# Tables and value/gate weights prepared behind the first queries and keys of an attention and expert layer, with queries and keys one slot earlier in the written order

## What is computed

```python
x = x + attn(layernorm(x), Wqg, Wkv, Wout)      # 16 heads, keys of 16, values of 64
x = x + ffn(layernorm(x), gate_kernel, gate_bias, w_gate, w_up, w_down, sw_gate, sw_up, sw_down)

# attn: q, k, v are L2-normed per head
q, g = split(x @ Wqg); k, v = split(x @ Wkv)
aggr = square(relu(q @ k.T)) @ v
out = tanh(|aggr|) * aggr / |aggr| * tanh(silu(g)); return out @ Wout
# ffn: 16 experts of 64, top 4 out of the best 2 of 4 groups, scaled by 2.5, and one shared expert of 128
y = sum_e combine[e] * ((silu(x @ w_gate[e]) * (x @ w_up[e])) @ w_down[e]) + shared(x)
```

## Time and profile before

| | us |
|---|---|
| median of 3 runs | 763.42 (762.53 to 763.88) |
| the profiled execution | 764.07 |
| its span, first to last instruction | 762.0 |
| PE busy in the span | 675.1 |
| DVE busy | 542.9 |
| ACT busy | 434.9 |
| POOL busy | 354.8 |
| mean granted clock of PE | 0.973 |

### The profile page before, as it was taken

The page is one execution under the profiler, slowest core; times in us unless marked ns, Lnnn a source line. Parts: engine busy times, 40 slices in busy tenths (PEclk is TensorE's granted clock), DMA queues, the critical chain, the costliest instruction groups (busy, mean ns, idle before and its releaser), DMA issues.

```text
span 762.0 us, 15278 instructions
## 1 busy us (share of the span) xinstructions
PE 675.1 (89%) x5160; PEld 519.9 (68%) x5160; DVE 542.9 (71%) x1739; ACT 434.9 (57%) x986; POOL 354.8 (47%) x368
## 2 busy tenths in 40 slices
PE   2658888999999999999999999999999999998876
PEld 1525456777777777777777778777777777666775
DVE  3526657788796868787886868687877968686652
ACT  3456757666567575666666675656566675543211
POOL 3225746464546454555546464554545463734000
PEclk9879999999999999999999999999999999999998
DMA  8699486657291929357481909284572919000000
GB/s 211 109 139 105 90 92 110 72 96 92 72 116 37 121 32 137 51 104 86 86 102 57 124 19 143 36 129 59 103 80 79 102 56 120 6 15 3 7 8 8
DMA packets 72830, 61.24 MB, mean 80 GB/s; under 512 B 8625, under 2 KB 72497, under 8 KB 72753
## 3 DMA queue, kind: packets, MB, share of 16 engines
q1 hardware_dynamic: 72752, 60.26, 53.8%
HBM read 41.37 MB, written 18.87 MB: 79 GB/s over the span
## 4 chain that ended last, share of the span: by engine, by line
PE 50%; DVE 27%; ACT 11%; issue 7%; DMA 3%; POOL 1%; SPq 1%; DVEq 0%; ACTq 0%; POOLq 0%
PE ps_a L493 9%; PE ps_f L437 9%; PE ps_f L418 8%; PE ps_f L355 5%; PE ps_s L464 4%; PE ps_f L357 4%; PE ps_f L356 4%; DVE it L841 4%; DVE norms_y L652 3%; DVE norms_t L651 3%; PE ps_f L397 3%; ACT qk_parts L546 2%; ACT r L592 2%; DMA qkt<-qk_rows 2%; ACT qk_sq L548 2%
## 5 line engine op out<-in xcount | busy, mean ns | idle before, releaser
L324 POOL TENSOR_TENSOR p<-r 128x512 f32<-128x512 f32 x256 | 264.2, 1053 | 322.9 <-ACT r L592 290.0
L592 ACT ACTIVATE r<-ps_s 128x512 f32<-128x512 f32 x256 | 139.6, 601 | 86.8 <-PE ps_s L464 83.0
L493 PE MATMUL ps_a<-p,v 128*64 128x256 f32 x1024 | 147.9, 400 | 4.0 <-POOL p L324 2.3
L493 PEld LDWEIGHTS ps_a<-p,v 128*64 128x64 f32 x1024 | 65.0, 138 | 45.2 <-POOL p L324 5.2
L584 ACT ACTIVATE it<-ps_f 128x256 f32<-128x256 f32 x144 | 55.6, 386 | 63.4 <-PE ps_f L357 60.3
L887 DVE TENSOR_TENSOR big<-ps_a,wt 128x256 f32<-128x256 f32 x128 | 53.7, 420 | 48.5 <-ACT big L601 47.2
L841 DVE TENSOR_TENSOR it<-ps_f,it 128x256 f32<-128x256 f32 x144 | 58.8, 419 | 28.9 <-ACT it L584 28.3
L464 PE MATMUL ps_s<-qkt 64*128 64x256 f32 x512 | 66.7, 335 | 9.4 <-DMA qkt<-qk_rows 7.4
L730 DVE TENSOR_REDUCE norms_m<-sq 128x8 f32<-128x512 f32 x64 | 43.7, 683 | 43.7 <-ACT sq L556 43.7
L437 PE MATMUL ps_f<-wdown,it 128*128 128x128 f32 x576 | 72.6, 288 | 1.3 <-DVE it L858 1.3
L437 PEld LDWEIGHTS ps_f<-wdown,it 128*128 128x128 f32 x576 | 70.0, 203 | 1.5 <-DVE it L858 1.5
(11 more groups left out here) (153 smaller groups left out, 1487.9 us busy)
## 6 DMA issues: line engine op xcount, KB each, us to landing
qk_rows<-qk_parts SPq DMA_DIRECT2D x16, 1024.0 KB, 4.4
qkt<-qk_rows SPq DMA_DIRECT2D x64, 256.0 KB, 9.9
qkt<-qk_rows SPq DMA_DIRECT2D x128, 128.0 KB, 9.3
x_in<-in_L_attn_tokens SPq DMA_DIRECT2D x16, 128.0 KB, 3.4
x_res<-in_L_attn_tokens SPq DMA_DIRECT2D x16, 128.0 KB, 14.1
out<-o_sb SPq DMA_DIRECT2D x16, 128.0 KB, 14.2
big<-in_L_attn_Wqg SPq DMA_DIRECT2D x1, 640.0 KB, 4.2
big<-in_L_attn_Wkv SPq DMA_DIRECT2D x1, 640.0 KB, 5.5
```

The costliest lines, as they stand in the source:

```text
L324: pool.tensor_tensor(p[h % 4][:], r[h % 2][:], r[h % 2][:], ALU.mult).then_inc(probs_done, 1)
L493: last = pe.matmul(ps_a[k % 2][64 * e:64 * e + 64, 0:N], v[s % 3][:, t, h * DV:(h + 1) * DV], p[h % 4][:, t * N:(t + 1) * N], start=(t == ...
L592: act.activation(r[h % 2][:], ps_s[h % 2][:], ACT.Relu).then_inc(relu_done, 1)
```

## The change

PE's list: in slot 5 qk 0 takes the place of v 0 (place 26, bank 2). In slot 6 qk 1 and v 0 take places 29 (bank 1) and 30 (bank 2), v 1 takes 32 (bank 0). In slot 7 v 2 takes 34 (bank 2); v 3 stays at 36. x2T, at 38, now shares its bank with v 2, v 0 with qk 0. DVE's order follows: low part 0 in slot 5, low part 1 and sums 0 and 1 in slot 6, sums 2 and 3 in slot 7.

At the start PE and ACT wait for less (the identity, one constant; Wqg and Wkv each under a semaphore of its own). POOL builds the other nine tables in slot 1 of step -2, behind its first root. ACT copies the high parts of value and gate weights behind the evacuation of qk 1 of step -2. DVE makes the low parts of query and key weights behind xn, those of value and gate weights in slot 6 behind low part 1, followed by the cast of sel. PE waits for all tables at the head of step -1, ACT behind its copies.

```diff
--- before.py
+++ after.py
@@ -48,9 +48,9 @@
         [("P", "g", 2), ("F", "gu", 5), ("F", "cT", 0), ("F", "gu", 6), ("O", "rT", 0)],
         [("O", "rB", 0), ("O", "rB", 1), ("F", "gu", 7), ("O", "rB", 2), ("L", "xT", 0), ("O", "rB", 3), ("P", "g", 3),
          ("F", "gu", 8)],
-        [("O", "y", 0), ("L", "v", 0), ("O", "y", 1), ("F", "cB", 0)],
-        [("L", "v", 1), ("L", "qk", 0), ("F", "cB", 1), ("L", "v", 2), SKIP],
-        [("L", "qk", 1), ("F", "cB", 2), ("L", "v", 3), ("F", "cB", 3), ("O", "x2T", 0), SKIP],
+        [("O", "y", 0), ("L", "qk", 0), ("O", "y", 1), ("F", "cB", 0)],
+        [("L", "qk", 1), ("L", "v", 0), ("F", "cB", 1), ("L", "v", 1), SKIP],
+        [("L", "v", 2), ("F", "cB", 2), ("L", "v", 3), ("F", "cB", 3), ("O", "x2T", 0), SKIP],
     ]
     ORDER = [job for slot in FILL for job in slot]
     assert len(FILL) == SLOTS and len(ORDER) % 4 == 0
@@ -166,7 +166,7 @@
 
 
         x_loaded, x_back = ([sem(f"{name}{q}") for q in range(2)] for name in ("x_loaded", "x_back"))
-        w_loaded = [sem(f"w_loaded{k}") for k in range(3)]
+        w_loaded = [sem(f"w_loaded{k}") for k in range(4)]
         c_loaded = sem("c_loaded")
         out_stored = sem("out_stored")
         consts_pool, consts_dve = sem("consts_pool"), sem("consts_dve")
@@ -215,7 +215,7 @@
 
             load_x(0, 0)
             sp.dma_start(big[:, 0:HK + HV], Wqg).then_inc(w_loaded[0], 16)
-            sp.dma_start(big[:, HK + HV:2 * (HK + HV)], Wkv).then_inc(w_loaded[0], 16)
+            sp.dma_start(big[:, HK + HV:2 * (HK + HV)], Wkv).then_inc(w_loaded[3], 16)
             load_x(1, 1)
             base = raw_experts
             for w, sw in ((w_gate, sw_gate), (w_up, sw_up)):
@@ -291,25 +291,27 @@
             built(pool.memset(ident[:], 0.0))
             built(pool.affine_select(out=ident[:], in_=ident[:], compare_op=ALU.not_equal, fill=1.0, base=0,
                                      pattern=[[-1, P]], channel_multiplier=1))
-            built(pool.memset(selraw, 0.0))
...
+            def tables():
+                built(pool.memset(selraw, 0.0))
...
             def root(dst, src, ready):
                 pool.tensor_tensor(dst[:], src[:], minus_half[:].broadcast_to([P, T]), ALU.pow).then_inc(ready, 1)
@@ -325,6 +327,8 @@
                     if k == 1 and "L" in on:
                         pool.wait_ge(ch_l, 3 * (s + 3))
                         root(rstd1, var1, rstd1_ready)
+                    if k == 1 and at == FIRST_STEP:
+                        tables()
                     if k == 6 and "O" in on:
                         pool.wait_ge(ch_n, 3 * s)
                         root(rstd2, var2, rstd2_ready)
@@ -345,8 +349,7 @@
 
         @block.tensor
         def _(pe):
-            pe.wait_ge(consts_pool, 12)
-            pe.wait_ge(consts_dve, 2)
+            pe.wait_ge(consts_pool, 3)
 
             weights = {"qk": 2, "v": 3, "g": 4, "gu": 6, "lg": 7, "y": 7, "y2": 7}
 
@@ -369,13 +372,13 @@
                     for t in range(T):
                         last = pe.transpose(ps[:, tok[t]], xn[:, t, :], ident[:])
                 elif kind == "qk":
+                    if j == 0:
+                        pe.wait_ge(xh_ready, b + 1)
+                        pe.wait_ge(read["xT"], b + 1)
                     for c in range(2):
                         cols = slice(j * HK + c * P, j * HK + (c + 1) * P)
                         last = three(ps[:, c * N:(c + 1) * N], (wqk[0][:, cols], wqk[1][:, cols]), (xh[xb][:], xl[xb][:]))
                 elif kind == "v":
-                    if j == 0:
-                        pe.wait_ge(xh_ready, b + 1)
-                        pe.wait_ge(read["xT"], b + 1)
                     half = slice((j % 2) * 512, (j % 2 + 1) * 512)
                     last = three(ps[:, :], (xh[xb][:, tok[j // 2]], xl[xb][:, tok[j // 2]]), (wv[0][:, half], wv[1][:, half]))
                 elif kind == "g":
@@ -468,6 +471,9 @@
                             last.then_inc(scores_done, 1)
 
             def step(s, q, on, at):
+                if at == FIRST_STEP + 1:
+                    pe.wait_ge(consts_pool, 12)
+                    pe.wait_ge(consts_dve, 3)
                 n = 0
                 for k in range(SLOTS):
                     for stage, kind, j in FILL[k]:
@@ -501,9 +507,9 @@
         @block.scalar
         def _(act):
 
-            act.wait_ge(consts_pool, 3)
-            act.activation(carrier2[:], ident[0:1, 0:1], ACT.Silu)
-            act.wait_ge(w_loaded[0], 32)
+            act.wait_ge(consts_pool, 1)
+            act.activation(carrier2[:], minus_half[0:1, 0:1], ACT.Silu)
+            act.wait_ge(w_loaded[0], 16)
             gq = big[:, 0:HK + HV].rearrange("p (h c) -> p h c", h=H)
             kv = big[:, HK + HV:2 * (HK + HV)].rearrange("p (h c) -> p h c", h=H)
             base = raw_experts
@@ -512,10 +518,13 @@
                 return w.rearrange("p (h c) -> p h c", c=c)
 
             act.activation(heads(wqk[0][:, 0:HK], DK), gq[:, :, 0:DK], ACT.Copy).then_inc(w_hi, 1)
+            act.wait_ge(w_loaded[3], 16)
             act.activation(heads(wqk[0][:, HK:2 * HK], DK), kv[:, :, 0:DK], ACT.Copy).then_inc(w_hi, 1)
-            act.activation(heads(wv[0][:], DV), kv[:, :, DK:], ACT.Copy).then_inc(w_hi, 1)
-            act.activation(heads(wg[0][:], DV), gq[:, :, DK:], ACT.Copy).then_inc(w_hi, 1)
-            act.wait_ge(consts_dve, 2)
+
+            def value_weights():
+                act.activation(heads(wv[0][:], DV), kv[:, :, DK:], ACT.Copy).then_inc(w_hi, 1)
+                act.activation(heads(wg[0][:], DV), gq[:, :, DK:], ACT.Copy).then_inc(w_hi, 1)
+                act.wait_ge(consts_dve, 3)
 
             def expert_weights():
                 act.wait_ge(w_loaded[1], 32)
@@ -602,6 +611,8 @@
                     for stage, kind, j in FILL[k]:
                         if stage in on:
                             evacuate(stage, kind, j, s, q)
+                        if (kind, j) == ("qk", 1) and at == FIRST_STEP:
+                            value_weights()
                         if (kind, j) == ("gu", 4) and "O" in on:
                             act.wait_ge(n_ready, s)
                             act.activation(nn[:], nn[:], ACT.Tanh).then_inc(tanh_n, 1)
@@ -677,8 +688,6 @@
                 ins.then_inc(consts_dve, 1)
                 dve.wait_ge(consts_dve, n[0])
 
-            dve.wait_ge(consts_pool, 12)
-            dve.tensor_copy(sel[:], selraw)
             dve.memset(rt[:].bitcast(F32), 0.0)
             dve.memset(ct[:].bitcast(F32), 0.0)
             dve.memset(ones32[:], 0.0)
@@ -704,11 +713,16 @@
                     lo, hi = lo.rearrange("p (h c) -> p h c", c=c), hi.rearrange("p (h c) -> p h c", c=c)
                 dve.tensor_tensor(lo, raw, hi.bitcast(F32), ALU.subtract).then_inc(w_lo, 1)
 
-            def projection_weights():
+            def query_key_weights():
                 rest(1, [w[:, 0:HK] for w in wqk], gq[:, :, 0:DK], DK)
                 rest(2, [w[:, HK:2 * HK] for w in wqk], kv[:, :, 0:DK], DK)
+
+            def value_weights():
                 rest(3, [w[:] for w in wv], kv[:, :, DK:], DV)
                 rest(4, [w[:] for w in wg], gq[:, :, DK:], DV)
+                dve.wait_ge(w_lo, 4)
+                dve.wait_ge(consts_pool, 12)
+                built(dve.tensor_copy(sel[:], selraw))
 
             def expert_weights():
                 rest(5, [w[:] for w in weg], big[:, base:base + FC * P], 0)
@@ -941,13 +955,12 @@
                         if P_on:
                             value_scales(link_p, s + 1, rq2[pq])
                             link_p.end()
-                        if at == FIRST_STEP:
-                            projection_weights()
-                            dve.wait_ge(w_lo, 4)
                         if L_on:
                             wait(dve, done["xT"], s + 2)
                             dve.wait_ge(rstd1_ready, s + 3)
                             normed_rows(x_in[q], mv1, rstd1, xn, ln1_ready)
+                        if at == FIRST_STEP:
+                            query_key_weights()
                         if F:
                             gate_up([6])
                     if k == 4:
@@ -975,7 +988,7 @@
                             dve.wait_ge(x_back[pq], (b - pq) * 8 + 16)
                             residual_row(0)
                         if L_on:
-                            sums(0, s + 2)
+                            low_parts(0, s + 2)
                         if O:
                             residual_row(1)
                             dve.wait_ge(read["y"], 2 * b + 2)
@@ -986,8 +999,11 @@
                     if k == 6:
                         gated_heads(k)
                         if L_on:
-                            sums(1, s + 2)
-                            low_parts(0, s + 2)
+                            low_parts(1, s + 2)
+                        if at == FIRST_STEP:
+                            value_weights()
+                        if L_on:
```

(12 more changed lines are left out.)

26 lines of the change are left out of this document (16 added, 10 removed).

## The result

| | before | after |
|---|---|---|
| median of 5 runs | 763.13 us (762.53 to 763.88) | 754.61 us (753.53 to 755.82) |
| the profiled execution | 764.07 | 755.62 |
| its span | 762.0 | 753.6 |
| PE / DVE / ACT / POOL busy | 675.1 / 542.9 / 434.9 / 354.8 | 680.0 / 543.5 / 431.8 / 354.3 |

The ratio is 0.989, with an interval from 0.9875 to 0.9905: faster by 8.5 us. The forecast was 752.5, 2.1 us too low.

The account below looks back on a forecast made before the run. It took PE to bound the middle steps, and the query-key store and loads, not engine work, the start. Terms -7.1 + 2.6 - 6.5 = -11.0 on the 763.42 median gave 752.5 us; own range 749.5 to 755.5, 8-in-10 range 747 to 759.5.

Parts of the forecast that it names:

- the likeliest case: Whole kernel: the forecast itself, 752.5 us, chance 0.48.
- The 0.4: Step -1 at the start: gains another 0.4 us, as its second product no longer waits for the first low part.
- Start: Up to batch 0's first ReLU: it comes at 43.6 instead of 50.68 us, -7.1 us.
- The tables beside DVE: Before the first product: POOL's tables beside xn and key weights' low parts cost 0 to 2 us, taken as +1.0.
- rival F: At the start: POOL's tables hold DVE for the full 2 us, total 753.5 us; chance 0.12.
- Step 0: Step 0: v0 waits for a low part behind the experts' weights, PE idle about 5 us, +2.6 us.
- Middle steps: Step 1 and twelve middle steps: x2T starts 0.71 us earlier, y2 0.48 a step, -6.5 us in all.
- rival E: Middle steps: y2 is not held by DVE and keeps the full 0.71 us, total 749.7 us; chance 0.08.
- The last steps: Kernel's end, where code doesn't change: the prediction had no term, so 0 us.
- B: Middle steps: another wait takes x2T's place and they gain nothing, total 759.0 us; chance 0.15.
- C: Start gains nothing: store held in the queue or slower loads, scores again near 50 us, total 759.5; chance 0.10.
- D: Slot 6 of every step: v0 waits for DVE as in step 0, total 772 us, slower; chance 0.07.

Follow-up runs that it names:

- the order alone: The kernel before with only the new list of jobs and DVE's matching order, constants and weights prepared as before: 757.93 us, 0.9936 of the kernel before.
- all three edits: Changed kernel, step 0's low part before experts' weights, fourth hidden tile before last sum, value/gate weights before query-key evacuations: 746.36 us, again 749.62.
- fourth tile first: The changed kernel, but in slot 7 DVE scales the fourth hidden tile ahead of the last sum of value squares: 753.21 us, 0.987 of the kernel before.
- the preparation alone: The changed kernel with the old job list and DVE order, keeping the later tables and weight parts: 760.05 us, 0.996 of the kernel before.

## Why the prediction was right, and where it was off

The direction, the mechanism of each part and the likeliest case held; the sizes of four terms were off, partly against each other. The start came out 1.2 us better, step 0, the middle and the end 0.9, 1.6 and 1.4 worse. That the total missed by only 2.1 is in part luck.

**Start, -7.1 forecast, -8.3 measured.** By its marks: first product 9.7 forecast, 9.47 measured; store 14.75, 14.25; values from 18.1, 17.59; the last of them done near 23.0, at 22.73. Until here the walk is right to half a microsecond. The mis-sized step is step -1: from the end of the values to the tanh it took 17.5 us where it took 18.8 before, so it gained 1.3 and not 0.4.

The 0.4 itself was right: from the first evacuation of queries or values to the tanh it is 6.96 us against 7.37, here and with the order alone. What failed is "by the same lengths". xn ends 1.25 us behind DVE's instruction before it (line 778, the values' scales) where it ended 2.20 behind it: it now follows that one without a gap (0.32 before), starts ahead of POOL's multiplication, and takes 1.32 instead of 1.89. That belongs to the preparation: all ten kernels with it have 1.23 to 1.25, the kernel before and the order alone 2.20 and 2.21. Why xn had the gap before and not now isn't known.

The loads were 0.75 us later than forecast (40.55 against 39.8), since the store landed at 19.70 and not 19.2, and they took 20.85 and not 20.65. They were late at no cost, as the forecast had it, but with less room than its 3 us: about 1.2.

**The tables beside DVE, +1.0 forecast, about 0.9 measured.** 0.34 on the two xn (0.94 against 0.60) and 0.87 on the second low part (1.29 against 0.42). The first is hidden, since xn ends at 6.07, ahead of the key weights at 7.25; the second is the cost. The Trainium skill (SBUF: State Buffer, section "Who interferes with whom") has a DVE instruction with two SBUF inputs contend with a GpSimd instruction that reads SBUF. The low part, which has two, stretched threefold beside the selections and was back at 0.42 with the tables moved; the first low part, which had begun (5.99) before the selections did (6.07), kept 0.41. Trace and rule agree. The lengthening of xn, whose one large input is x_in, is outside that sentence. The full 2 us that rival F drew from the rule did not come: all four operations together were 1.2 us longer.

**Step 0, +2.6 forecast, +3.5 measured.** The place, the wait (4.78 us against "about 5") and the releaser were right. The stall cost 1.85 us here, 0.75 less than the term, and 3.25 in two kernels with the same stall, both within the forecast's ends of 1.2 (full clock) and 3.5 (half clock). Which it is depends on how long the clock stays at half behind the idle time. What the sum lacked is another 1.6 us ahead of the stall: step 0 began at a granted clock of 0.68 instead of 0.77 in its first 10 us. At 0.77 to 0.83 that part took 24.8 to 25.0 us in four kernels, at 0.68 26.5, at 0.62 27.1. That the change brings this lower clock is not shown: three kernels with the new order have 0.78 to 0.83 there, and one and the same kernel (all three edits) had 0.78 and 24.9 us in one profile, 0.72 and 26.2 in the other.

**Middle steps, -6.5 forecast, -4.9 measured.** On the scale of the earlier trace rows x2T was forecast at 370.65 and came at 370.64, the fourth tile was to end at 373.09 and did; y2 was to start at 373.15, 0.06 behind it, and started at 373.24, 0.15 behind. That is the first thing mis-sized, 0.09. By the next slot 6 a further 0.06 is gone, so that a step gains 0.32 and not 0.48. Where that 0.06 goes was not looked for. That the fourth tile is what holds y2 (the ground for taking 0.48 and not 0.71) is shown by "fourth tile first", which gets 0.31 more; rival E falls with it.

**The last steps, 0 forecast, +1.4 measured.** The prediction had no term for code that doesn't change. Its clock isn't the same from one execution to the next, and this profile had a low one. Of the 1.4, 0.3 is the change's: from step 13's x2T to step 14's it is 39.54 us against 39.26, and 39.5 to 39.6 in every kernel with the new order and the fourth tile last (39.2 to 39.3 in the others). Step 14 has no products of queries or values, so (argued, not tested) the last of the x2T gain is given back there. The other 1.1 is no effect of the change that any run shows: the kernels with the same code there have a last part of 96.7 to 100.8 us.

**The rivals.** B (another wait takes x2T's place): in part, a third of the 0.48. C fell: the loads release the scores but not the ReLU; with the preparation alone they do hold it, though at 46.55 and not near 50. D fell: v0's product waits for a low part for 4.78 us in step 0 and 0.68 in step -1 (35.15 us), and not in the middle, where steps fell to 41.87. The total of 754.61 lies between the forecast and B, inside the forecast's own range.

## What to carry to other kernels

A job's place in a rotating list of buffers decides whose reader it waits for; before moving one, write out the new neighbour in each bank, in the middle steps and in the first ones, where another engine's one-time work can stand in front of that reader. A one-time block costs nothing only where nobody waits for what is queued behind it: moving one small instruction ahead of it gave 2.0 us here by the marks (3.2 between the medians), about a quarter of what the whole change brought. And when a wait is removed, look at once for the next operand that is late, since moving the fourth tile in front of a sum nobody waited for doubled the gain of the steps.

## What was not expected of the hardware

- **The end of the kernel has no fixed time.** In the last 100 us, with the same code, one execution took 96.7 and another 100.8 us, in step with the granted clock of stretches in which PE is partly idle. Runs of one kernel differ by up to 5.9 us (744.26 at 0.979, 750.13 at 0.968), mostly for it, so that a gain under 1% is read better from marks inside the profile (the mean step of kernels with the same steps repeated to 0.02 us) than from five totals. The Trainium skill (TensorE: Matmul & The Clock Gate, section "Part 1: The HAM clock gate (the "warmup" mystery)") has PE that idles fall to 1.2 GHz, and the trace agrees: 0.50 in the 4 us behind the 4.8 us stall with the order alone. What no row here tells is why the same 4.8 us are followed by 0.64 in one kernel and 0.50 in another.
- **Whoever begins first sets whom the overlap of DVE and POOL costs.** Nine kernels build the tables beside the low parts of the query and key weights, and the order differs from profile to profile. In three DVE's first low part began 0.05 to 0.08 us ahead of POOL's first selection: it took 0.40 to 0.43 us and the selection 1.35 to 1.41. In six the selection began first, by 0.05 to 0.31: it took 1.17 and the low part 1.13 to 1.39. The prediction read its two prices of xn, 0.60 and 1.89, as POOL quiet and POOL busy; with POOL busy but begun later it is 1.32.
- **A store behind other loads isn't much slower.** 5.45 us against 4.44, with the experts' weights ahead of it in the queue. Rival C needed some 10 us more at the scores.
- **ACT's recorded length isn't its pace.** From 358.23 to 363.76 it works without a gap, and the recorded length of its 512-column instructions grows from 0.60 to 0.74 us (0.71 for the square at 362.80), while each goes on for some 0.48 us until the next starts. Such a stretch is costed by its starts, and only its last instruction by its length: x2T starts at 363.57, 0.06 behind the square's recorded end.
